# Expert rows stored as planes of 16-bit halves and loaded with transposing transfers, in a transformer layer on one core

## What is computed

```python
x = L0_attn_x                                    # (8, 256, 256)
x = x + attention(layernorm(x))                  # q, k, v, rotary, causal softmax, output
x = x + moe(layernorm(x))

def moe(x):                                      # T = 2048 rows, H = 256, E = 8, I = 176
    scores = softmax(x @ gate_w.T)
    topk_w, topk_idx = top_k(scores, 2); topk_w /= sum(topk_w)
    y_e = (silu(x @ w1[e]) * (x @ w3[e])) @ w2[e]         # for each expert e
    y = sum over the row's two experts of topk_w * y_e
    return y + silu(x @ sw1) * (x @ sw3) @ sw2            # the shared network, twice as wide
```

## Time and profile before

| | |
|---|---|
| Median of 3 runs | 731.71 us (731.58 to 732.68) |
| The profiled execution, its time | 731.76 us |
| Its span | 729.7 us |
| TensorE busy | 714.3 us (98%) |
| VectorE busy | 616.6 us (85%) |
| ScalarE busy | 527.1 us (72%) |
| POOL busy | 507.0 us (69%) |

### The profile page before, as it was taken

One profiled execution on the slowest core, in us unless ns is written; L12 is line 12 of the kernel. 1 busy time (PEld: TensorE's weight loads), 2 busy tenths in 40 slices (PEclk: granted clock), 3 DMA queues, 4 the chain that ended last, 5 costly groups with the idle time before them and its releaser, 6 DMA issues.

```text
span 729.7 us, 16434 instructions
## 1 busy us (share of the span) xinstructions
PE 714.3 (98%) x5465; PEld 687.1 (94%) x5465; DVE 616.6 (85%) x1773; ACT 527.1 (72%) x1664; POOL 507.0 (69%) x531
## 2 busy tenths in 40 slices
PE   5999999999999999999999999999999999999997
PEld 5999999999999999999999989999999989999997
DVE  6888899989998989898989887989898966776557
ACT  5787777777777777677777776777777765666564
POOL 4997467787778777877787777777866623544545
PEclk9999999999999999999999999999999999999999
DMA  6664214221422143213312331121454374344382
GB/s 204 172 185 153 81 31 140 108 93 29 140 106 90 41 140 118 77 56 132 131 61 63 127 116 37 45 97 38 147 193 157 143 257 130 118 120 133 103 300 99
DMA packets 51212, 85.91 MB, mean 118 GB/s; under 512 B 8633, under 2 KB 43417, under 8 KB 49529
## 3 DMA queue, kind: packets, MB, share of 16 engines
q1 hardware_dynamic: 47080, 73.44, 30.4%
q0 software_dynamic: 4048, 11.42, 4.4%
HBM read 60.12 MB, written 44.59 MB: 143 GB/s over the span
## 4 chain that ended last, share of the span: by engine, by line
PE 87%; DVE 5%; POOL 4%; issue 1%; DMA 1%; ACT 1%; SPq 0%; POOLq 0%; DVEq 0%
PE bank L659 65%; PE bank L709 5%; PE bank L699 4%; PE bank L718 3%; DVE work L1098 2%; POOL work L486 2%; PE bank L951 1%; PE bank L932 1%; PE bank L846 1%; DVE work L1091 1%; POOL qkt_lo L1781 1%; PE bank L701 1%; PE bank L907 1%; PE bank L963 1%; PE bank L967 1%
## 5 line engine op out<-in xcount | busy, mean ns | idle before, releaser
L486 POOL TENSOR_TENSOR work<-work 128x512 f32<-128x512 f32 x127 | 165.0, 1299 | 51.8 <-DVE work L1098 48.7
L1781 POOL TENSOR_TENSOR qkt_lo<-work,qkt_hi 128x512 fp32r<-128x512 f32 x112 | 145.0, 1294 | 73.1 <-ACT qkt_hi L1539 73.1
L1098 DVE TENSOR_TENSOR work<-bank,sinn 64x512 f32<-64x512 f32 x256 | 176.2, 688 | 3.4
L659 PE MATMUL bank<-xnt_hi,w_lo 128*128 128x256 f32 x512 | 149.0, 291 | 1.9 <-DVE xnt_lo L1423 1.0
L659 PE MATMUL bank<-xnt_lo,w_hi 128*128 128x256 f32 x512 | 145.6, 284 | 0.0
L659 PE MATMUL bank<-xnt_hi,w_hi 128*128 128x256 f32 x512 | 145.5, 284 | 0.0
L1539 ACT CAST qkt_hi<-work 128x512 fp32r<-128x512 f32 x112 | 69.6, 621 | 84.8 <-POOL work L486 84.5
L1546 ACT ACTIVATE work<-work,bias 128x128 f32<-128x128 f32 (+1 forms) x256 | 112.7, 441 | 0.5 <-DVE bias L1107 0.5
L1091 DVE TENSOR_TENSOR work<-bank,cosn 128x512 f32<-128x512 f32 x128 | 88.0, 687 | 20.7 <-PE bank L659 20.0
L659 PEld LDWEIGHTS bank<-xnt_hi,w_lo 128*128 128x128 f32 x512 | 98.5, 192 | 2.9 <-DVE xnt_lo L1423 1.4
L659 PEld LDWEIGHTS bank<-xnt_hi,w_hi 128*128 128x128 f32 x512 | 98.9, 193 | 0.4
(11 more groups left out here) (202 smaller groups left out, 2126.4 us busy)
## 6 DMA issues: line engine op xcount, KB each, us to landing
rows_by_expert<-in_zero_t SPq DMA_DIRECT2D x17, 1028.0 KB
weights_split<-stage SPq DMA_DIRECT2D x40, 176.0 KB, 1.9
w_lo<-weights_split SPq DMA_DIRECT2D x4, 1408.0 KB, 9.8
w_lo<-results_by_token SPq DMA_DIRECT2D x16, 256.0 KB, 5.4
w_lo<-rows_by_expert SPq DMA_DIRECT2D x24, 128.5 KB, 2.1
w_hi<-weights_split SPq DMA_DIRECT2D x2, 1536.0 KB, 6.8
stage<-in_L_ffn_w SPq DMA_DIRECT2D x32, 88.0 KB, 2.1
weights_split<-stage SPq DMA_DIRECT2D x20, 128.0 KB, 2.0
```

The source lines that it names most:

```text
L486: eng.tensor_tensor(roped[:, a], rope_cos[:, a], rope_sin[:, a], ALU.add).then_inc(rope_add, 1)
L659: mm = pe.matmul(out, lhs[a], rhs[b], start=start and n == 0, stop=stop and n == 2, skip_group_check=more)
L1098: op = nc.vector.tensor_tensor(rope_sin[lo:lo + 64, a], p_qk[a][hi:hi + 64, :, :], sn, ALU.mult)
L1781: nc.gpsimd.tensor_tensor(qkt[a][1][:, :, :], roped[:, a], qkt[a][0][:, :, :], ALU.subtract).then_inc(qkt_lo, 1)
```

## The change

In HBM a row of `rows_by_expert` keeps its 257 words, but the 256 numbers are stored as two planes of 16-bit halves: first the 256 low halves, then the 256 high halves. ScalarE makes these planes (`halves`): once per sequence for sequences 1 to 6 into `xn` behind head 11, for the rows sent during the last sequence into `late_rows` behind its head 8, and for the last rows twice among the expert tiles, for the two copies of them (behind tiles 5 and 8; before there was one copy of plain words behind tile 5). `xn` now holds the rows being sent, and `xn2` only the normed ones.

SyncE loads a tile with two DMAs on one semaphore: a transposing one (`dma_start_transpose`), which puts 128 rows x 512 halves as 128 partitions x 4 x 128 halves, and a plain one with the 128 place words. There are 6 places instead of 12, and the load of tile j waits until tile j-6 is joined. VectorE joins the halves to words (`merge_x`: the destination is written in steps of two halves); ScalarE makes the upper part from these words in SBUF, VectorE the lower. `turn_x` goes, and TensorE doesn't touch the rows before `up_e`. On POOL, the fourth scatter of a sequence moves from head 15 to head 0 of the next, the second place and the third scatter from head 14 to head 15, and a wait for all scatters at head 1 goes; VectorE's `compare` waits for them instead.

```diff
+HSLOTS = 6
-        xn = sb("xn", [P, ST, D])
+        xn = sb("xn", [P, ST, RW])
...
-        x_slot = [stage_all[:, n * RW:(n + 1) * RW] for n in range(NEAR)]
-        x_slot += [whl[1][:, far + n * RW:far + (n + 1) * RW].bitcast(F32) for n in range(ESLOTS - NEAR)]
+        x_slot = [stage_all[:, n * D:(n + 1) * D] for n in range(NEAR)]
+        x_slot += [stage_all[:, rows_at + DC * P:rows_at + DC * P + D], work[:, 0:D]]
+        x_halves = [t.bitcast(U16).rearrange("p (k s) -> p k s", k=2 * DC) for t in x_slot]
+        x_place = [work[:, 840 + n:841 + n] for n in range(ESLOTS)]
+        x_words = [work[:, 2560:2816], work[:, 1728:1984]]
+        late_rows = stage_all[:, 0:ST * RW].rearrange("p (t d) -> p t d", t=ST)
+        def sent_rows(n):
+            return late_rows if n == B - 1 else xn
...
             def tile_in(j):
-                if j == NEAR:
-                    sp.wait_ge(y_ps, B * N)
+                if j >= HSLOTS:
+                    sp.wait_ge(x_merged, j - HSLOTS + 1)
...
-                sp.dma_start(x_slot[j % ESLOTS], xs_d[bass.ds(row, P), :]).then_inc(x_got[j % ESLOTS], 16)
+                sp.dma_start_transpose(x_halves[j % HSLOTS], xs_halves[bass.ds(row, P), 0:2 * D]).then_inc(x_got[j % HSLOTS], 16)
+                    sp.dma_start(x_place[j % ESLOTS], xs_d[bass.ds(row, P), D:RW]).then_inc(x_got[j % HSLOTS], 16)
...
-            def turn_x(j):
-                if j >= 1:
-                    pe.wait_ge(xe_lo, j)
-                pe.wait_ge(x_got[j % ESLOTS], 16 * (j // ESLOTS + 1))
-                for c in range(DC):
-                    mm = pe.transpose(p_xe[:, c, :], x_slot[j % ESLOTS][:, c * P:(c + 1) * P], ident[:, :])
-                mm.then_inc(xe_ps, 1)
...
             for j in range(NJ):
-                if j + 1 < NJ:
-                    turn_x(j + 1)
...
+            def merge_x(j):
+                dve.wait_ge(x_got[j % HSLOTS], 32 * (j // HSLOTS + 1))
+                nc.vector.tensor_copy(x_words[j % 2].bitcast(U16).rearrange("p (s two) -> p two s", two=2),
+                                      x_halves[j % HSLOTS].rearrange("p (two c) s -> p two (c s)", two=2)).then_inc(x_merged, 1)
+
             def low_x(j):
                 dve.wait_ge(xe_hi, j + 1)
-                nc.vector.tensor_tensor(xe_t[1][:, j % 2], p_xe[:, 0:DC, :], xe_t[0][:, j % 2],
+                nc.vector.tensor_tensor(xe_t[1][:, j % 2], x_words[j % 2].rearrange("p (c s) -> p c s", c=DC), xe_t[0][:, j % 2],
...
             mult_s(3)
+            merge_x(0)
             low_x(0)
             low_s(2)
+            merge_x(1)
...
                 if j + 1 < NJ:
                     low_x(j + 1)
+                if j + 2 < NJ:
+                    merge_x(j + 2)
...
+                    if b is LAST and h == 8:
+                        for a in range(2):
+                            act.wait_ge(kept[a], kept_count(NP - NATT - 2 + (NP - NATT + a) % 2))
+                        halves(b, sent_rows(b))
+                    if b is not FIRST and b is not LAST and h == 11:
+                        halves(b, sent_rows(b))
...
             def high_x(j):
-                act.wait_ge(xe_ps, j + 1)
-                nc.scalar.copy(xe_t[0][:, j % 2], p_xe[:, 0:DC, :]).then_inc(xe_hi, 1)
+                act.wait_ge(x_merged, j + 1)
+                if j >= 2:
+                    act.wait_ge(ue_ps, j - 1)
+                nc.scalar.copy(xe_t[0][:, j % 2], x_words[j % 2].rearrange("p (c s) -> p c s", c=DC)).then_inc(xe_hi, 1)
...
-            def copy_rows():
-                act.wait_ge(xn2_done, B)
-                nc.scalar.copy(twin[:, :, 0:D], xn2[:, :, 0:D]).then_inc(twin_done, 1)
+            def halves(n, rows):
+                act.wait_ge(xn2_done, n)
+                nc.scalar.copy(rows[:, :, 0:D].bitcast(U16).rearrange("p t (two d) -> p t two d", two=2),
+                               xn2[:, :, :].bitcast(U16).rearrange("p t (d two) -> p t two d", two=2)).then_inc(halves_done, 1)
...
                 if j == TURN + 2:
-                    copy_rows()
+                    halves(B, twin)
+                if j == GATE + 4:
+                    act.wait_ge(pick_done, B)
+                    halves(B, xn)
...
-                        if h == 1:
-                            wait(pool, scattered, 64 * (b - 1))
+                        if h == 0 and b > 1:
+                            send(sent_rows(b - 1)[:, 1, :], 1, 1)
```

More of the change, by code:

```diff
@@ L12 @@
 I32 = mybir.dt.int32
+U16 = mybir.dt.uint16
 ALU = mybir.AluOpType
@@ L331, in build @@
         ys_add = sem("ys_add")
-        x_got = [sem(f"x_got{a}") for a in range(ESLOTS)]
-        xe_ps = sem("xe_ps")
+        x_got = [sem(f"x_got{a}") for a in range(HSLOTS)]
+        x_merged = sem("x_merged")
         xe_hi = sem("xe_hi")
@@ L588, in tile_in @@
                                      max_val=XROWS - P, skip_runtime_bounds_check_because="a tile of the list")
-                sp.dma_start(x_slot[j % ESLOTS], xs_d[bass.ds(row, P), :]).then_inc(x_got[j % ESLOTS], 16)
+                sp.dma_start_transpose(x_halves[j % HSLOTS], xs_halves[bass.ds(row, P), 0:2 * D]).then_inc(x_got[j % HSLOTS], 16)
+                with nc.allow_non_contiguous_dma(reason="a word of each row"):
+                    sp.dma_start(x_place[j % ESLOTS], xs_d[bass.ds(row, P), D:RW]).then_inc(x_got[j % HSLOTS], 16)
             for g in range(G):
@@ L1253, in rows_norm @@
                 dve.wait_ge(rstd2_done, n)
+                wait(dve, halves_done, n - 1)
                 for t in range(ST):
@@ L1260, in compare @@
                 dve.wait_ge(logit_done, n)
+                if n < B:
+                    wait(dve, scattered, 64 * (n - 1))
                 scores = pair[:, 1, :].rearrange("p (t e) -> p t e", t=ST)
@@ L1827, in sequence @@
                             pool.wait_ge(routed, b * RP - 1)
-                            send(xn2[:, 0, :], 0, 0)
+                            pool.wait_ge(halves_done, b)
+                            send(sent_rows(b)[:, 0, :], 0, 0)
                         if b is LAST and h == 11:
-                            send(xn2[:, 1, :], 0, 1)
+                            send(sent_rows(b)[:, 1, :], 0, 1)
                         if b is LAST and h == 12:
@@ L1838, in sequence @@
                         if b is not LAST and h == 13:
-                            send(xn2[:, 1, :], 0, 1)
-                        if h == 14:
+                            send(sent_rows(b)[:, 1, :], 0, 1)
+                        if h == 15:
                             pool.wait_ge(own_done, 3 * b - 1)
-                            send(xn2[:, 0, :], 1, 0)
-                        if h == 15:
-                            send(xn2[:, 1, :], 1, 1)
+                            send(sent_rows(b)[:, 0, :], 1, 0)
+                            next_own(b)
                             pool.wait_ge(xt_stored, 16 * b)
@@ L1900, in first_place @@
                 wait(pool, own_done, 3 * (n - 1))
-                nc.gpsimd.tensor_copy(xn2[:, :, D].bitcast(I32), own[:, :]).then_inc(own_done, 1)
+                if n == LAST:
+                    pool.wait_ge(halves_done, n)
+                nc.gpsimd.tensor_copy(sent_rows(n)[:, :, D].bitcast(I32), own[:, :]).then_inc(own_done, 1)
             def second_place(n):
                 pool.wait_ge(scattered, 64 * n - 32)
-                nc.gpsimd.tensor_scalar(xn2[:, :, D].bitcast(I32), own[:, :], 1.0, 1.0, ALU.add,
+                nc.gpsimd.tensor_scalar(sent_rows(n)[:, :, D].bitcast(I32), own[:, :], 1.0, 1.0, ALU.add,
                                         ALU.mult).then_inc(own_done, 1)
@@ L1913, in send @@
                 nc.gpsimd.indirect_dma_start(
-                    out=xs_d, out_offset=bass.IndirectOffsetOnAxis(ap=slot[:, c, t:t + 1], axis=0),
-                    in_=row, in_offset=None).then_inc(scattered, 16)
+                    out=xs_d.bitcast(I32), out_offset=bass.IndirectOffsetOnAxis(ap=slot[:, c, t:t + 1], axis=0),
+                    in_=row.bitcast(I32), in_offset=None).then_inc(scattered, 16)
             def results_out(j, tiles):
@@ L1920, in results_out @@
                 nc.gpsimd.indirect_dma_start(
-                    out=res_d, out_offset=bass.IndirectOffsetOnAxis(ap=x_slot[j % ESLOTS][:, D:RW].bitcast(I32), axis=0),
+                    out=res_d, out_offset=bass.IndirectOffsetOnAxis(ap=x_place[j % ESLOTS].bitcast(I32), axis=0),
                     in_=y_slot[j % YSLOTS], in_offset=None).then_inc(y_out[j % YSLOTS], 16)
@@ L1942, in _ @@
                 sequence(b)
-            pool.wait_ge(scattered, 64 * (B - 1))
             rsqrt(mv2_done, vare2_done, rstd2_done, B, ST)
-            for c, rows in enumerate((xn2, twin)):
-                op = nc.gpsimd.tensor_scalar(rows[:, :, D].bitcast(I32), own[:, :], float(c), 1.0, ALU.add, ALU.mult)
-            op.then_inc(own_done, 1)
             results_out(0, 1)
@@ L1956, in _ @@
             choose(B)
+            for c, rows in enumerate((xn, twin)):
```

(2 more changed lines are left out.)

30 lines of the change are left out of this document (13 added, 17 removed).

## The result

The changed kernel takes 746.18 us (median, 745.52 to 747.38) against 732.36 for the kernel before in the same comparison: a ratio of 1.0193, with a 95% interval of 1.018 to 1.0206. It is slower by 1.9%, 13.8 us, where 2.4 us less were forecast; 746.2 is also above the upper end of the range, 742.

The account below looks back on a forecast made before the run. TensorE was taken to bound the kernel, full in the attention stage and among expert tiles. The sum 8.4 - 3.0 - 0.6 - 0.8 - 1.1 - 0.5 = 2.4 us less gave 729.3 us, with a range of 726.6 to 742.

Parts of the forecast that it names:

- part 5: SyncE's loads of expert tiles: two loads and an address take 1.25 us a tile, below 1.78; 1.1 us charged at tile 21.
- rival on small pieces: Expert-tile loads: transposing loads move 512 small pieces, 2.11 us a tile, 738.5 us; chance 0.16, shared with a pace-setting issue.
- Part 1: TensorE, expert tiles: it loses the turn of 39 tiles, 38 x 0.22 = 8.4 us gained.
- Part 2: VectorE, expert tiles: a joining copy of 512 halves adds 0.35 us a round, exposing single jobs; 3.0 us charged.
- rival with one element at a time: VectorE's joining copy costs 0.62 us and sets a pace of 1.86 us; 3.0 us slower, 734.8; chance 0.14.
- part 4: Entry to the expert tiles: joining and splitting the first tile's halves comes 0.8 us late, with nothing hiding it.
- Part 3: ScalarE, expert tiles: two copies of 1024 halves, about 1.07 us each, overrun by 0.3 each; 0.6 us charged.
- Part 6: Attention stage: ScalarE's copies of 1.07 us have 1.4 us of cover, POOL's moved scatter is covered; 0.5 us charged.
- Tile 21: First tile of the second list: its load lands 1.5 or 0.7 us late and VectorE stands; 1.1 us charged.
- loads one after another: Expert-tile loads: each transposing load starts only when one has landed; 773 us, or about 738 with 2.1 us landing; chance 0.12.

Follow-up runs that it names:

- experiment 1: Changed kernel with a plain load in place of each tile's transposing load: 731.2 us, ratio 0.9988 to the kernel before.
- experiment 2: Changed kernel with the transposing load taking two of a tile's four blocks, the upper halves alone: 745.8 us, ratio 1.018 to the kernel before.
- experiments 6 and 7: Changed kernel with plain loads, plus two or one one-word transfers a tile on SyncE: 742.9 us with two, 735.5 us with one.
- experiment 8: Changed kernel with plain loads and without VectorE's joining copy: 725.3 us, ratio 0.9905 to the kernel before.
- experiment 4: Changed kernel with the place words loaded from POOL's queue in place of SyncE's: 737.0 us, ratio 1.0064 to the kernel before.

## Why the prediction failed, step by step

**The step that failed is part 5**, the pace of SyncE. It said: "With a second one, and its address, I estimate 1.25 us, below 1.78." The estimate took the transposing instruction's issue to be that of a plain one, 0.33 us. It measured 1.21, whatever its size (1.19 for half), and the place words 0.43 where 0.33 had been taken. A tile then holds SyncE 2.28 us and TensorE 1.78. Even for plain loads the estimate was short: with them experiment 1 shows 1.36 to 1.43. I wrote that "the trace shows nothing" of the transposing load, and weighed other values for its landing, its packets and its overlap, but took a single one for its issue. The prediction has an issue that sets the pace only in a few words beside the rival on small pieces, whose 738.5 us are worked out from packets; its own price was open. Experiments 1, 2, 6 and 7 show the cause: taking the transposing load away gives 15.0 us back, halving its data nothing, and putting the time back on SyncE without any transposing brings back 11.7 of the 15.0.

**Part 1** (8.4 us from TensorE) was right in mechanism: with SyncE and the copy out of the way the round is 1.78 us, and the kernel 725.3, 6.9 us under the kernel before, with ScalarE's copies still charged. In the changed kernel the gain shows as idle time of TensorE.

**Part 2** had the copy right and its effect too small. The copy is at the low end, as chosen:
```profile
L1323 DVE COPY work<-stage x33: 445/463/651, 599.7 to 695.0; 128x512 uint16<-128x512 uint16 x33
```
From one start to the next it is 0.34 us. The rival with one element at a time is gone; two elements a cycle, the rule of the Trainium skill ("VectorE: DVE Perf Modes", "Walkthrough: the 8-slice pipeline in each mode"), fits the trace. But the sum charged 3.4 us for it with its half of part 4, and experiment 8 measures 5.8. Jobs of 0.6 us do not spread over rounds: they stand in single ones, which overrun (2.13 us), as the sum foresaw; that accounts for some 2.0 us. Where the rest comes from is read from two traces and not tested: the waits of the copy for its load, at tile 21 and behind it, and the entry.

**Part 3** said 1.07 us for each of ScalarE's large copies:
```profile
L1707 ACT COPY xn<-xn x7: 1050/1053/1057, 146.4 to 625.7; 128x1024 uint16<-128x1024 uint16 x7
```
The length is right. No run took the two copies of the tile stage away by themselves, so their 0.6 us is not tested.

**Part 4, the entry,** was 0.8 us, and the rows show it (TensorE, before and at the first tile):
```profile
599.58 0.49 PE L920 MATMUL bank<-ident,work 128*128 128x128 f32 x3
601.21 0.42 PE L672 MATMUL bank<-w_lo,qkt_lo 128*128 x1 [1.14 <-issue]
```
The wait is 1.14 us where it was 0.22: 0.92 more.

**Part 6** charged 0.5 us for the attention stage, and no run can tell it from nothing. The first tile starts at 601.21 against 601.15 although its wait is 0.92 longer, so what comes before it ended 0.86 us earlier; 0.22 of that is the first tile's turn, which left this place. But with the same attention stage the first tile starts at 601.50 in experiment 1 and at 601.80 in experiment 2, so the remaining 0.6 is no more than such starts differ by.

**Tile 21** was the second part of part 5. The list ends on VectorE in the first row and the copy starts in the second; between them SyncE issues the load at 650.11, in the third:
```profile
649.39 0.18 DVE L1413 SCALAR_TENSOR_TENSOR mask<-work 128x18 int32<-128x18 f32 x1
...
653.38 0.60 DVE L1323 COPY work<-stage 128x512 uint16<-128x512 uint16 x1 [1.94 <-DMA work<-rows_by_expert]
```
```profile
650.11 1.20 SPq L600 DMA_TRANSPOSE stage<-rows_by_expert  x1
```
The stall is 1.94 us, of which 1.1 were charged, and 653.38 - 650.11 = 3.3 us lie between the issue and the copy. It is released by the place words, but they are not the reason: in experiment 4, where the copy waits for the transposing load alone, the stall is 2.13 us and the distance from the issue 3.5. With plain loads it is 0.94 (experiment 1).

**The whole.** The kernel stood at 746.2. With plain loads it is 731.2 (experiment 1), 1.2 us under the kernel before; my sum, which left the issue's excess out, was 2.4 under it. The loads one after another did not happen, though the pace would have looked alike: in experiment 4 they leave as close as 1.62 us apart, and land 2.6 to 4.8 us after their issue. The Trainium skill's figure of 1309 ns for a transposing transfer of 128 x 128 halves ("VectorE: DVE Perf Modes", "The three transpose paths") is near the 1.21 us that one instruction holds its queue here, but here that price is for four blocks and for two alike, so four times the figure is not what the trace shows.

**Not settled:** what the attention stage gained or lost, what the shared semaphore costs by itself, and how short SyncE's issue would have to be for the change to pay. The runs with plain loads put that between 1.43 us a tile (731.2, 1.2 under the kernel before) and 1.96 (735.5, 2.9 over it). No version of these runs with transposing loads beats the kernel before.

## What to carry to other kernels

When an instruction of a kind that the trace does not have is put on a queue, bound what it costs the engine that issues it just as carefully as what it costs the engine it relieves, with a stage's pace worked out for both ends. List the queues of SyncE and the others as engines with a round of their own (issues, addresses, gaps), since the page's budget leaves them out, and compare that round with the bound engine's. And between a producer and a consumer that meet by way of a third engine, leave other work: an order that looks kinder to one instruction can put the trip in the open.

## What the runs showed of the hardware

- A transposing load issued by SyncE holds its queue for 1.21 us with four blocks of 128 x 128 halves, and 1.19 with two; a plain load of the same bytes 0.33 (experiment 1), one of a single word 0.24 to 0.39 (experiments 6 and 7).
- Its landing comes 2.6 to 4.2 us after its issue, with a median of 2.8, and doesn't hold up the next one: in experiment 4, with loads as close as 1.62 us, it is 2.6 to 4.8 with a median of 3.1.
- VectorE's copy of 512 halves in SBUF with a stride of two on the output lasts 0.46 us and delays the next instruction by 0.34, as much as an instruction of 256 words that reads PSUM (0.35 in the earlier trace rows).
- A transfer of 128 single words holds POOL's queue for 0.57 us (experiment 4), and SyncE's for 0.43, or 0.33 where the loads beside it are plain (experiment 1).
